# Moving the value products behind the side stages within each tick of a recurrent attention kernel

## The chip, the cores and the metric

The kernel runs on one core of a Trainium2 chip, as one program. The metric is the device time of one execution in microseconds. TensorE is called PE here, VectorE DVE, ScalarE ACT, GpSimd POOL and SyncE SP, as in the profile. PE's clock is granted at one of two levels, 1.2 or 2.4 GHz, which the profile shows as 0.5 or 1.0.

## The reference

The input is x, 16 sequences of 256 tokens with 128 features, all float32. Two layers each compute x = x + s * silu(g), where s is an attention and g a feed-forward stage of the normalized x.

```python
# layer 0
xn = layernorm(x)
s = attention0(xn)        # causal softmax attention, 16 heads of 64, then Wo and bo
g = silu(moe0(xn))        # one of 8 experts per token by a router, F = 352, plus a shared expert
x = x + s * g
# layer 1
xn = layernorm(x)
s = linear_attention(xn)  # 16 heads of 8, phi = elu + 1, cumulative sums of k*v over the tokens
g = silu(local_transformer(xn))
x = x + s * g
# local_transformer: 2 layers; token shift, qkv (8 heads of 64), l2norm of q and k, rotary with
# scale, softmax over a window of 64 and its predecessor, wo, residual; then
# token shift, layernorm, GLU with gelu (341), down projection, residual
```

## The kernel before

Tokens lie on the 128 partitions. Two sequences (512 tokens, four tiles of 128) make a block; there are 8 blocks. Both softmax attentions are cut into steps. A step is one pair of heads (`i`, 0 to 3), one sequence of the block (`s`, 0 or 1) and one part (half of the heads, or layer). Two steps with the same `i` make a pair. There are 256 steps in a plan of 361 ticks that is laid out when the kernel is built. Some ticks have no step, because the next layer's input isn't there yet.

A step passes through a pipeline of ticks. In tick T, PE makes the q of the pair that starts in T+2 and the k of the pair that starts in T+1 (`produce`, L488 or L498), the logits of step T (L508, L511), the transposes of the probabilities of step T-1 (L519) and the value products of step T-2 (`values`, L534, L537). If that was the second step of its pair, PE also transposes the expanded reciprocal sums, so that they lie as the output does (`merge`, L544). DVE masks and scales the logits and takes the maximum (L921), copies the transposed probabilities (L932), inverts the sums (L938) and multiplies the values by the reciprocals (`scaled`, L943), the last one tick later. ACT copies q and k (L758), takes the exponentials (L780, L781) and copies the spread of the reciprocals (`merge`, L758, tile rT). POOL expands the reciprocals (L1220).

All other work is in side stages, which the plan puts on ticks: `route` and the experts (`eT` L592, `eg` L603 and L608, `ed` L618), the value projection `v` (L479), the output projection `wo` (L562), the shared expert (`ffn`, `down0` L577, `comb`), and for layer 1 `xT`, `lin` (L630 on PE, L1070 and L1071 on DVE), `qkv` (three matmuls of 128x512 for one tile, L636; ACT squares and copies the first two banks, L836 and L837, DVE sums the squares, L1108, and applies the tables, L1113, POOL does L1302 and L1303, DVE `rot` L1118, then `rr`), `cum` (the cumulative sums: L645 and L647 on PE, L1086 and L1089 on DVE), `oT`, `s1`, `shift`, `ln2`, `yT`, `glu` (L682 and L684, ACT L858, DVE L1136), `down1` (L691, DVE L1142), `hT` and `fin` (L1148 to L1152). On every engine a tick is the attention's pipeline steps followed by the tick's side stages, with one exception that the change is about: where in this order `values` and `merge` stand.

The order of each engine's work is its program order, written out by the loops over the ticks. Engines wait for each other by semaphores. PSUM's eight banks are four rings of two: mm (q, k, the spread, and those side results that ACT reads), s (the logits, and side results that DVE reads), pt (transposed probabilities) and o (the value products). `count_units` walks the plan once and numbers the uses of each ring. A use waits until the use two before it in its ring was read. These numbers have to follow the order in which PE and the readers do the work, which is why `count_units` is changed with the loops.

Of the kernel before, what the change touches and what calls it, by code (L numbers as in the profile page):

```python
# [401 lines left out]
def count_units(c, plan):  # L402

    mm, s, pt, o = (Ring(f, d, 2) for f, d in ((c.mm_full, c.mm_done), (c.s_full, c.s_done),
                                                (c.pt_full, c.pt_done), (c.pv_done, c.o_done)))
    rings = {"mm": mm, "s": s, "pt": pt}
    for i in range(BLOCKS):
        mm.add(("rT", i))
    for t in range(TILES):
        mm.add(("v", 0, 0, t))  # L410
    mm.add(("q", 0))
    mm.add(("k", 0))
    o.add(("scores",))
    o.add(("cum",))
    plan.combs, combs = {}, 0
    for tick in range(plan.length):
        if plan.starts(tick + 2):
            mm.add(("q", plan.step(tick + 2).pair))
        if plan.starts(tick + 1) and tick:
            mm.add(("k", plan.step(tick + 1).pair))  # L420
        if st := plan.step(tick):
            for h in range(2):
                s.add(("s", st.n, h))
        if st := plan.step(tick - 1):
            for h in range(2):
                pt.add(("t", st.n, h))
        if st := plan.step(tick - 2):
            if st.s == 0:
                o.add(("o", st.pair))
            else:  # L430
                mm.add(("m", st.pair))
        for seg in plan.side.get(tick, ()):
            for ring, n in USES.get(seg[0], {}).items():
                for j in range(n):
                    rings[ring].add((*seg, j))
            plan.combs[seg] = combs
            combs += seg[0] == "comb"
    return mm, s, pt, o


# [12 lines left out]
def tensor(nc, pe, c, plan, mm, s, pt, o):  # L453
    MM, LAST = nc.tensor.matmul, PAIRS - 1

    def mm_bank(*name):
        if mm.free(*name):
            pe.wait_ge(c.mm_done, mm.free(*name))
        return c.mm_ps[mm.slot(*name)]
# [22 lines left out]
    def produce(which, st):  # L482
        bank = mm_bank("qk"[which], st.pair)
        if st.kind == 0:
            a = (st.part * PAIRS + st.i) * P
            if st.part == 0 and st.i == 0 and which == 0:
                pe.wait_ge(c.mm_done, mm.done("rT", st.b) if st.b < 2 else mm.done("xnT", st.b, 0))
            MM(bank[:, :], c.wqk[which][:, a:a + P], c.xnT[:, st.b % 2, :], start=True, stop=True).then_inc(c.mm_full, 1)  # L488
        else:
            if st.i == 0:  # L490
                g = LAYERS * st.b + st.part
                if which == 0:
                    pe.wait_ge(c.rot_ready, TILES * (g + 1))
                else:
                    pe.wait_ge(c.kn_ready, TILES * (g + 1))
            a = which * INNER1 + st.i * P
            for t in range(TILES):
                last = nc.tensor.transpose(bank[:, t * P:(t + 1) * P], c.qkr[:, t, a:a + P], c.ident[:, :])  # L498
            last.then_inc(c.mm_full, 1)

    def logits(st):
        if st.s == 0:
            pe.wait_ge(c.mm_done, mm.done("k", st.pair))
        banks = [s_bank("s", st.n, h) for h in range(2)]
        q, k = (c.qk[a][:, st.pair % 2, st.s * SEQ:(st.s + 1) * SEQ] for a in range(2))
        for h in range(2):
            f = HD * h
            MM(banks[h][:, 0:P], q[f:f + HD, 0:P], k[f:f + HD, 0:P], start=True, stop=True)  # L508
        for h in range(2):
            f = HD * h  # L510
            MM(banks[h][:, P:SB], q[f:f + HD, P:SEQ], k[f:f + HD, :], start=True, stop=True).then_inc(c.s_full, 1)  # L511

    def transposes(st):
        for h in range(2):
            u = 2 * st.n + h
            bank = pt_bank("t", st.n, h)
            pe.wait_ge(c.exp_done, u + 1)
            for j in range(3):
                last = nc.tensor.transpose(bank[:, j * P:(j + 1) * P], c.p[:, u % 4, j * P:(j + 1) * P], c.ident[:, :])  # L519
            last.then_inc(c.pt_full, 1)  # L520

    def values(st):
        bank = c.o_ps[o.slot("o", st.pair)]
        if st.s == 0:
            pe.wait_ge(c.o_done, o.free("o", st.pair))
            if st.i == 0:
                pe.wait_ge(c.mm_done, mm.done("qkv", st.b, st.part, LAST, 2) if st.kind else mm.done("v", st.b, st.part, LAST))
        v = (c.v0, c.v1)[st.kind][:, st.part, :, :]
        pe.wait_ge(c.pt_done, pt.done("t", st.n, 1))
        pts = [c.pt[:, (2 * st.n + h) % 4, :] for h in range(2)]  # L530
        q = st.s * SEQ
        for h in range(2):
            f, a = HD * h, st.i * P + HD * h
            MM(bank[f:f + HD, q:q + SEQ], v[:, 2 * st.s, a:a + HD], pts[h][:, 0:SEQ], start=True, stop=False)  # L534
        for h in range(2):
            f, a = HD * h, st.i * P + HD * h
            last = MM(bank[f:f + HD, q + P:q + SEQ], v[:, 2 * st.s + 1, a:a + HD], pts[h][:, SEQ:SB], start=False, stop=True)  # L537
        last.then_inc(c.pv_done, 1)

    def merge(pair):  # L540
        bank = mm_bank("m", pair)
        pe.wait_ge(c.rdx_ready, pair + 1)
        for t in range(TILES):
            last = nc.tensor.transpose(bank[:, t * P:(t + 1) * P], c.rdx[:, pair % 2, t * P:(t + 1) * P], c.ident[:, :])  # L544
        last.then_inc(c.mm_full, 1)
# [182 lines left out]
    for tick in range(plan.length):  # L728
        if plan.starts(tick + 2):
            produce(0, plan.step(tick + 2))  # L730
        if plan.starts(tick + 1) and tick:
            produce(1, plan.step(tick + 1))
        if plan.step(tick):
            logits(plan.step(tick))
        if plan.step(tick - 1):
            transposes(plan.step(tick - 1))
        if st := plan.step(tick - 2):
            values(st)
            if st.s == 1:
                merge(st.pair)  # L740
        if tick == 4:
            pe.wait_ge(c.wo_loaded, 16 * 2)
            pe.wait_ge(c.sh_loaded, 16 * 4)
            pe.wait_ge(c.p1_loaded, c.P1_LOADS)
        for seg in plan.side.get(tick, ()):
            if seg[0] in stage:
                stage[seg[0]](*seg[1:])


def scalar(nc, act, c, plan, mm, s, pt, o):  # L750
# [6 lines left out]
    def evacuate(dst, *name):  # L757
        A(dst, mm_bank(*name)[:, :], ACT.Copy).then_inc(c.mm_done, 1)  # L758
# [11 lines left out]
    def produce(which, st):  # L770
        evacuate(c.qk[which][:, st.pair % 2, :], "qk"[which], st.pair)

    def exps(st):
        if st.s == 0 and st.pair >= 2:
            act.wait_ge(c.rden_ready, st.pair - 1)
        for h in range(2):
            u = 2 * st.n + h
            act.wait_ge(c.s_done, s.done("s", st.n, h))
            den, p = c.den[:, st.pair % 2, 2 * st.s + h, :], c.p[:, u % 4, :]
            A(p[:, 0:P], p[:, 0:P], ACT.Exp, bias=c.nmax[:, u % 4, 0:1], scale=-1.0, accum_out=den[:, 0:1])  # L780
            A(p[:, P:SB], p[:, P:SB], ACT.Exp, bias=c.nmax[:, u % 4, 1:2], scale=-1.0, accum_out=den[:, 1:2])\  # L781
                .then_inc(c.exp_done, 1)

    def merge(pair):
        if pair >= 2:
            act.wait_ge(c.o_done, o.done("o", pair - 2))
        evacuate(c.rT[:, pair % 2, :], "m", pair)
# [89 lines left out]
    for tick in range(plan.length):  # L877
        if plan.starts(tick + 2):
            produce(0, plan.step(tick + 2))
        if plan.starts(tick + 1) and tick:  # L880
            produce(1, plan.step(tick + 1))
        if plan.step(tick):
            exps(plan.step(tick))
        if (st := plan.step(tick - 2)) and st.s == 1:
            merge(st.pair)
        if tick == 4:
            act.wait_ge(c.p1_loaded, c.P1_LOADS)
            act.wait_ge(c.hT_zero, 1)
        for seg in plan.side.get(tick, ()):
            if seg[0] in stage:  # L890
                stage[seg[0]](*seg[1:])


def vector(nc, dve, c, plan, mm, s, pt, o):
# [619 lines left out]
```

## Time and profile before

| | |
|---|---|
| median of 3 runs | 2476.11 us (2475.27 to 2476.41) |
| profiled execution | 2475.04 us |
| span in its profile | 2473.2 us |
| PE busy | 1920.5 us, 78% |
| DVE busy | 1487.3 us, 60% |
| ACT busy | 1093.3 us, 44% |
| POOL busy | 626.2 us, 25% |
| mean granted clock of PE | 0.888 |

The profile is one execution on the chip. Busy time is summed over an engine's instructions. A gap in front of an instruction is put down to the semaphore event that ended it, and the name behind `<-` is the instruction that raised it. In the timeline an engine's instructions of the same line are merged into one row; its first number is the start from the beginning of the span, its second the duration. The idle time in brackets is that ahead of the row's first instruction.

### The profile page before, as it was taken

What the parts mean: (1) busy time and instruction counts of PE and PEld (TensorE: products, weight loads), DVE (VectorE), ACT (ScalarE), POOL (GpSimd) and SP (SyncE); (2) the same over time, 40 slices, a digit from 0 to 9 for tenths busy, and PEclk for the clock granted to TensorE, in tenths of its full rate; (3) what the DMA queues carried; (4) which work ended last, traced back from release to release, by engine and by line L of the source; (5) the groups of instructions that cost most, each with busy time, mean ns of one, the idle gap of its engine ahead of it and who ended that gap; (6) DMA issues with size and microseconds to landing.
All of it is one profiled execution on the core that took longest, in us unless ns stands there. A gap on an engine that the chain in (4) does not pass through costs nothing.

```text
span 2473.2 us, 34580 instructions
## 1 busy us (share of the span) xinstructions
PE 1920.5 (78%) x11092; PEld 1219.0 (49%) x11092; DVE 1487.3 (60%) x4595; ACT 1093.3 (44%) x3143; POOL 626.2 (25%) x656
## 2 busy tenths in 40 slices
PE   5699977987689777887688676887699767866756
PEld 4377744554346445545355344544455435533524
DVE  4355557656665675646665656656666666566655
ACT  2355545454444454454344443454354444344334
POOL 2722223222411331131410323122321231034120
PEclk9799998998889898898889888998899788978878
DMA  7244300000000000000000000000000000000000
GB/s 215 79 153 159 116 8 1 1 5 1 1 9 1 5 1 1 9 1 5 0 10 1 5 1 1 9 1 1 1 10 1 1 1 5 1 5 0 5 1 5
DMA packets 46542, 51.69 MB, mean 21 GB/s; under 512 B 6290, under 2 KB 39068, under 8 KB 46364
## 3 DMA queue, kind: packets, MB, share of 16 engines
q0 software_dynamic: 7808, 27.79, 3.4%
q1 hardware_dynamic: 38556, 21.69, 3.1%
q8 instruction: 92, 1.51, 0.3%
q14 instruction: 86, 0.70, 0.1%
HBM read 40.03 MB, written 9.44 MB: 20 GB/s over the span
## 4 chain that ended last, share of the span: by engine, by line
PE 53%; DVE 19%; issue 12%; ACT 8%; POOL 7%; DMA 1%; DVEq 0%; SPq 0%; POOLq 0%; another core or an unknown queue 0%; ACTq 0%
PE ps L519 6%; PE ps L511 5%; PE ps L562 5%; PE ps L508 5%; PE ps L534 4%; PE ps L488 3%; PE ps L636 3%; DVE ss L1108 2%; PE ps L544 2%; PE ps L479 2%; PE ps L682 2%; POOL big L1206 2%; PE ps L691 2%; PE ps L645 2%; PE ps L684 2%
## 5 line engine op out<-in xcount | busy, mean ns | idle before, releaser
L780 ACT ACTIVATE p<-p,nmax 128x128 f32<-128x128 f32 x512 | 201.7, 394 | 531.6 <-DVE nmax L921 527.4
L1220 POOL COPY rdx<-rden 128x256 f32<-128x256 f32 x256 | 96.0, 404 | 1146.6 <-DVE rden L938 1117.8
L508 PE MATMUL ps<-k,q 64*128 64x128 f32 x1024 | 142.2, 355 | 227.7 <-DVE big L1086 102.1
L921 DVE CUSTOM_DVE_ANT_0 p<-ps,mask 128x128 f32<-128x128 f32 (+1 forms) x512 | 152.7, 354 | 217.1 <-PE ps L511 194.3
L921 DVE CUSTOM_DVE_ANT_0 p<-ps,mask,nrq 128x128 f32<-128x128 f32 (+1 forms) x512 | 183.2, 414 | 153.3 <-PE ps L511 153.1
L932 DVE COPY pt<-ps 128x384 f32<-128x384 f32 x512 | 260.8, 550 | 19.8 <-PE ps L519 19.7
L508 PEld LDWEIGHTS ps<-k,q 64*128 64x128 f32 x1024 | 91.8, 210 | 358.3 <-issue 182.5
L519 PE MATMUL ps<-ident,p 128*128 128x128 f32 x1536 | 260.4, 312 | 6.6 <-DVE ff L969 3.9
L781 ACT ACTIVATE p<-p,nmax 128x256 f32<-128x256 f32 x512 | 252.2, 493 | 0.0
L519 PEld LDWEIGHTS ps<-ident,p 128*128 128x128 f32 x1536 | 191.3, 157 | 111.7 <-issue 102.2
L636 PE MATMUL ps<-wqkv,hT 128*128 128x512 f32 x384 | 207.2, 645 | 49.5 <-ACT big L837 47.7
L498 PE MATMUL ps<-ident,big 128*128 128x128 f32 x512 | 94.9, 318 | 174.9 <-POOL big L1206 94.2
L1302 POOL TENSOR_TENSOR big<-big,rots 128x512 f32<-128x512 f32 x64 | 133.2, 2081 | 329.2 <-DVE ss L1108 329.2
L534 PE MATMUL ps<-pt,v 128*64 128x256 f32 x1024 | 187.2, 448 | 0.0
L511 PE MATMUL ps<-k,q 64*128 64x256 f32 x1024 | 182.7, 430 | 0.0
L498 PEld LDWEIGHTS ps<-ident,big 128*128 128x128 f32 x512 | 71.0, 165 | 207.7 <-issue 198.5
L758 ACT ACTIVATE q<-ps 128x512 f32<-128x512 f32 x128 | 76.0, 594 | 202.6 <-PE ps L498 114.5
L758 ACT ACTIVATE k<-ps 128x512 f32<-128x512 f32 x128 | 75.9, 593 | 181.5 <-PE ps L498 130.9
L1108 DVE TENSOR_REDUCE ss<-big 128x16 f32<-128x1024 f32 x64 | 77.9, 1217 | 105.7 <-ACT big L837 105.7
L562 PE MATMUL ps<-wo,attT 128*128 128x128 f32 x1024 | 133.8, 295 | 8.8 <-DVE attT L943 8.8
L636 PEld LDWEIGHTS ps<-wqkv,hT 128*128 128x128 f32 x384 | 62.7, 195 | 154.8 <-ACT big L837 102.6
L562 PEld LDWEIGHTS ps<-wo,attT 128*128 128x128 f32 x1024 | 132.3, 212 | 13.3 <-issue 12.4
(208 smaller groups left out, 3800.2 us busy)
## 6 DMA issues: line engine op xcount, KB each, us to landing
slots_in<-xn SPq DMA_DIRECT2D x1, 2560.0 KB, 14.0
v<-slots_in SPq DMA_DIRECT2D x20, 128.0 KB, 4.8
slots_out<-v SPq DMA_DIRECT2D x20, 128.0 KB
big<-in_x SPq DMA_DIRECT2D x4, 512.0 KB, 6.1
x<-in_x SPq DMA_DIRECT2D x8, 256.0 KB, 3.9
out_x<-x SPq DMA_DIRECT2D x8, 256.0 KB, 2.3
wqkv<-in_wqkv SPq DMA_DIRECT2D x2, 768.0 KB
g<-in_g SPq DMA_DIRECT2D x2, 341.0 KB
```

Of the source, the lines that this page charges most:

```text
L498: last = nc.tensor.transpose(bank[:, t * P:(t + 1) * P], c.qkr[:, t, a:a + P], c.ident[:, :])
L508: MM(banks[h][:, 0:P], q[f:f + HD, 0:P], k[f:f + HD, 0:P], start=True, stop=True)
L511: MM(banks[h][:, P:SB], q[f:f + HD, P:SEQ], k[f:f + HD, :], start=True, stop=True).then_inc(c.s_full, 1)
L519: last = nc.tensor.transpose(bank[:, j * P:(j + 1) * P], c.p[:, u % 4, j * P:(j + 1) * P], c.ident[:, :])
L534: MM(bank[f:f + HD, q:q + SEQ], v[:, 2 * st.s, a:a + HD], pts[h][:, 0:SEQ], start=True, stop=False)
L562: last = MM(bank[:, t * P:(t + 1) * P], c.attT[kind][:, i, t * P:(t + 1) * P], w, start=i == 0, stop=i == LAST)
L636: MM(bank[:, :], c.hT[:, t * P:(t + 1) * P], c.wqkv[:, l, i * INNER1:(i + 1) * INNER1], start=True, stop=True).then_inc(c.mm_full, 1)
L758: A(dst, mm_bank(*name)[:, :], ACT.Copy).then_inc(c.mm_done, 1)
L780: A(p[:, 0:P], p[:, 0:P], ACT.Exp, bias=c.nmax[:, u % 4, 0:1], scale=-1.0, accum_out=den[:, 0:1])
L781: A(p[:, P:SB], p[:, P:SB], ACT.Exp, bias=c.nmax[:, u % 4, 1:2], scale=-1.0, accum_out=den[:, 1:2])\
L921: last = V.tensor_tensor_reduce(out=c.p[:, u % 4, a:b], in0=bank[:, a:b], in1=c.mask[st.kind][:, P * (1 - i):SEQ], scale=scale, scalar=3e3 ...
L932: V.tensor_copy(c.pt[:, u % 4, :], bank[:, 0:SB]).then_inc(c.pt_done, 1)
```

## The change

On PE, `values` and `merge` are issued at the end of a tick, behind the side stages, and no longer ahead of them. On ACT, the copy of the spread moves behind the side stages too. In `count_units` the spread's number in the mm ring is given out behind those of the tick's side stages; the value products' ring (o) has the same order as before. DVE, POOL and SP are as they were: DVE's `scaled` still runs one tick after `values`, and POOL still expands the reciprocals at the start of its tick.

```diff
@@ count_units
-        if st := plan.step(tick - 2):
-            if st.s == 0:
-                o.add(("o", st.pair))
-            else:
-                mm.add(("m", st.pair))
+        if (st := plan.step(tick - 2)) and st.s == 0:
+            o.add(("o", st.pair))
         for seg in plan.side.get(tick, ()):
...
             combs += seg[0] == "comb"
+        if (st := plan.step(tick - 2)) and st.s:
+            mm.add(("m", st.pair))
@@ tensor
             transposes(plan.step(tick - 1))
-        if st := plan.step(tick - 2):
-            values(st)
-            if st.s == 1:
-                merge(st.pair)
         if tick == 4:
...
         for seg in plan.side.get(tick, ()):
             if seg[0] in stage:
                 stage[seg[0]](*seg[1:])
+        if st := plan.step(tick - 2):
+            values(st)
+            if st.s == 1:
+                merge(st.pair)
@@ scalar
             exps(plan.step(tick))
-        if (st := plan.step(tick - 2)) and st.s == 1:
-            merge(st.pair)
         if tick == 4:
...
                 stage[seg[0]](*seg[1:])
+        if (st := plan.step(tick - 2)) and st.s == 1:
+            merge(st.pair)
```

## Rows read from the trace of the kernel before

**Rows 1.** The page: PE's busy share, the chain by engine, PE's 40 slices.
```profile
PE 1920.5 (78%) x11092; PEld 1219.0 (49%) x11092; DVE 1487.3 (60%) x4595; ACT 1093.3 (44%) x3143; POOL 626.2 (25%) x656
...
PE   5699977987689777887688676887699767866756
...
PE 53%; DVE 19%; issue 12%; ACT 8%; POOL 7%; DMA 1%; DVEq 0%; SPq 0%; POOLq 0%; another core or an unknown queue 0%; ACTq 0%
```

**Rows 2.** Waits of the whole run: total us, times, longest us.
```profile
DVE ss L1108 <- ACT big L837: 105.7, 44, 4.3
...
PE ps L508 <- DVE big L1086: 102.1, 43, 7.0
...
PE ps L508 <- DVE v L1071: 68.5, 29, 3.8
...
PE ps L636 <- ACT big L837: 47.7, 54, 5.6
...
PE ps L508 <- DVE ff L1136: 5.6, 6, 0.9
...
PE ps L488 <- ACT xnT L758: 5.1, 6, 1.2
...
PE ps L508 <- DVE xb L1142: 2.2, 5, 0.4
```

**Rows 3.** Groups by line: busy us, mean ns, then idle us ahead.
```profile
L534 PE MATMUL ps<-pt,v 128*64 128x256 f32 x1024 | 187.2, 448 | 0.0
...
L544 PE MATMUL ps<-ident,rdx 128*128 128x128 f32 x512 | 89.6, 301 | 8.2 <-POOL rdx L1220 7.4 <-ACT hT L764 0.2
L943 DVE TENSOR_TENSOR attT<-ps,rT 128x512 f32<-128x512 f32 x128 | 82.9, 648 | 2.0 <-ACT rT L758 1.8
```

**Rows 4.** Timeline of ticks 115 and 116, first-layer qkv projection, block 2.
```profile
889.66 0.87 PE L519 MATMUL ps<-ident,p 128*128 128x128 f32 x6
...
890.47 0.65 PE L534 MATMUL ps<-pt,v 128*64 128x256 f32 x4
...
891.76 3.38 PE L636 MATMUL ps<-wqkv,hT 128*128 128x512 f32 x6
...
892.30 0.57 ACT L758 ACTIVATE rT<-ps 128x512 f32<-128x512 f32 x1
892.88 0.60 ACT L836 ACTIVATE big<-ps 128x512 f32<-128x512 f32 x1
...
895.21 1.22 DVE L1108 TENSOR_REDUCE ss<-big 128x16 f32<-128x1024 f32 x1 [3.10 <-ACT big L837]
...
899.64 0.80 PE L508 MATMUL ps<-k,q 64*128 64x128 f32 x4 [3.85 <-DVE v L1071]
...
901.22 1.54 PE L519 MATMUL ps<-ident,p 128*128 128x128 f32 x6
...
904.74 0.60 ACT L836 ACTIVATE big<-ps 128x512 f32<-128x512 f32 x1 [0.73 <-PE ps L636]
...
906.84 1.22 DVE L1108 TENSOR_REDUCE ss<-big 128x16 f32<-128x1024 f32 x1 [1.19 <-ACT big L837]
```

**Rows 5.** Timeline of ticks 138 and 139: value products, GLU, the next logits.
```profile
1058.67 0.65 PE L534 MATMUL ps<-pt,v 128*64 128x256 f32 x4
...
1059.47 1.11 PE L682 MATMUL ps<-xT,g 128*114 128x512 f32 x2
...
1065.81 0.49 PE L508 MATMUL ps<-k,q 64*128 64x128 f32 x4 [0.93 <-DVE ff L1136]
```

**Rows 6.** Timeline rows of ticks 8, 129 and 149.
```profile
118.44 0.66 PE L592 MATMUL ps<-ident,v 128*128 128x128 f32 x2 [12.74 <-DMA v<-slots_in]
...
996.13 0.80 PE L508 MATMUL ps<-k,q 64*128 64x128 f32 x4 [6.21 <-DVE big L1086]
...
1155.32 0.69 DVE L974 TENSOR_TENSOR ff<-ps,xn 128x512 f32<-128x512 f32 x1 [1.99 <-PE ps L577]
```

**Rows 7.** Windows view, PE alone: us, busy us (instructions), granted clock, DMA share, GB/s.
```profile
899.40:902.80 3.40, 3.16 (x16) 0.50 0.00 0
```

## The prediction

> **What bounds the kernel now.** I read the views in this order: the page's busy shares and chain, the totals of who waited for whom, the groups by line, and then single ticks in the timeline. TensorE (PE) is busy 78% of the span and holds 53% of the chain that ended last; in the third to fifth slice of the page it is at 9 tenths [rows 1]. That is the expert stage (ticks 9 to 29): PE has no idle time there, so an order that does the same work cannot gain in it. Elsewhere PE idles some 550 us in all (2473.2 less 1920.5). The reader is to see in the totals where it idles: at the logits of the next tick, L508, for a scores bank that VectorE (DVE) has not yet emptied of a side stage's result, 102.1 us behind the cumulative sums (L1086) and 68.5 us behind the linear attention's projection (L1071); and inside the qkv projection (L636), 47.7 us for ScalarE's (ACT) copies. DVE in turn waits 105.7 us for ACT's copies of that projection before L1108 [rows 2]. So PE, DVE and ACT hand one side stage to each other, and the tick ends when that relay ends. Against this stand the value products and their spread: L534 has 0.0 us of waits ahead of it over 1024 instructions, L544 has 8.2 us over 512, and DVE's consumer L943 waits 2.0 us over 128 [rows 3]. They are ready early and wanted late: filler that now stands ahead of the relay.
>
> **What moves.** In every tick PE's value products (0.80 us from L534's start to the next stage's, 1058.67 to 1059.47) [rows 5], and in every second one also the four transposes of the spread (1.29 us together, 890.47 to 891.76) [rows 4], go behind the side stages; ACT's copy of the spread, 0.57 us [rows 4], goes behind ACT's side stages; and the ring of matmul banks is numbered anew. No instruction is added or removed, no DMA is issued in the moved code, DVE's, POOL's and SP's orders stay. PE's work between two logits is the same, so a tick can only gain where PE, DVE or ACT waited for the side stage, and can only lose where the side stage, now earlier by 0.80 or 1.29 us, meets something that isn't ready and the filler no longer covers it.
>
> **First-layer qkv projection (4 ticks in each of 8 blocks).** Rows 4 show two of them. In the first, transposes end at 890.53. ACT's exponentials end at 892.30, then comes the spread's copy, and the projection's first copy L836 starts at 892.88. After the change the first bank is full by about 891.6 (one of the three in 3.38 us), so L836 can start at 892.30: 0.58 us earlier, and DVE's L1108, which waited 3.10 us, with it, and so the logits at 899.64, which waited 3.85 us for the last DVE step of the tick. PE itself ends later: its third bank needs the first one's copies, then filler follows, by my count at 5.9 us behind the transposes where it is 5.3 now; the 3.85 us hide that. In the second tick L836 waits 0.73 us for PE and L1108 1.19 us for ACT: 0.73 us gained [rows 4]. The third repeats the first, the fourth is bound by DVE and POOL: nothing. Per block 0.58 + 0.73 + 0.58 = 1.9 us, times 8 = 15 us (between 1.2 and 3 us per block, since the same ticks at half clock have more room: 10 to 24).
>
> **Second-layer projection (7 blocks with steps around it).** DVE waits on average 105.7 / 44 = 2.4 us in front of L1108 [rows 2], in the first of those ticks with the value products ahead; everything behind runs DVE, POOL, DVE. One 0.80 us each: 5.6 us (0 to 9).
>
> **Smaller relays.** The GLU tick ends in a wait of 0.93 us of the logits, with value products of 0.80 us ahead of the GLU [rows 5]; such waits sum to 5.6 us, those behind the down projection to 2.2 us, those of the next q for xnT's copy to 5.1 us, of which about 3.6 us have filler to cover them [rows 2]. Together 11.4 us. Behind the cumulative sums 43 waits make 102.1 us, but some 15 of them are of the kind of 996.13: 6.21 us, because DVE has 6 us of other work (the block's output) queued ahead of L1086, which the change doesn't touch [rows 2, 6]; 102.1 - 15 x 6.21 leaves 9 us, of which I take half, 4.5 us. Behind L1071, 15 of 29 are those of 3.85 us already counted [rows 2, 4]; of the remaining 11 us I take 2.5. Where the attention output and the shared down projection share a tick (the tick of 1155.32) DVE waits 1.99 us at L974, and then has three long steps before the next scores [rows 6]; 1.3 us in each of five such ticks: 6.5 us. Sum of gains: 15 + 5.6 + 11.4 + 4.5 + 2.5 + 6.5 = 45.5 us.
>
> **Losses.** (1) In the ten value-projection ticks outside the expert stage (L479, the shape of L636), PE fills two banks in 2.0 us behind the transposes, but ACT's exponentials end 1.77 us behind them and its first copy 0.6 us later [rows 4]: 0.4 to 0.5 us of wait that the filler covered, 5 us in all (0 to 13: with all 1.29 us lost). (2) The first expert transposes wait 12.74 us for a DMA, with value products ahead [rows 6]. They will run behind it, at half clock: 1.2 us (0.8 to 1.6). (3) A cumulative sum's bank is freed by DVE's first scores, some 0.1 us later than PE will come in about 20 ticks: 3 us (0 to 5). (4) Where yT is transposed, the next q or k waits for yT's copy instead of the spread's, 0.2 us x 7 = 1.4 us. Together 10.6 us. The delayed copy of the spread itself costs nothing: its reader L943 runs behind the next tick's scores and copies; if that cover were gone, it would be the side stage's length on DVE.
>
> **The sum.** 45.5 - 10.6 = 35 us. The profiled execution took 2475.04 us (span 2473.2), 1.1 us under the median of 2476.11; the difference carries over: 2476.1 - 35 = 2441 us.
>
> **Rivals.**
> (a) *The clock adds to it.* The stretch behind the 3.85 us wait is granted 0.50, the 1.2 GHz level [rows 7], and the six transposes there take 1.54 us where they took 0.87 a tick earlier [rows 4]. Filler in those waits makes them shorter by 1.3 us. If the clock then stays at 2.4 GHz, each such stretch gives back half of its 3.16 us of work, 1.6 us; two per block: 16 x 1.6 = 25 us more, 2416 us. The Trainium skill (TensorE: Matmul & The Clock Gate, "HAM oscillation") says that idle gaps between bursts throttle the array, and counts the penalty as half the throttled time; by that rule the trace agrees in the stretch shown, and the time would be this rival's. Against it: the waits that remain are still 2.5 to 6 us. Chance 0.15.
> (b) *Swallowed.* The gains meet DVE's or POOL's long steps later in the block (as at 996.13) and only a third arrives: 15 - 10.6 = 5 us, 2471 us. For it: DVE is busy 60% of the span and is what L508 waits for. Chance 0.15.
> (c) *Slower: the projection ticks become PE's.* In some 44 qkv ticks PE now stalls ahead of the third bank, because ACT is still in the exponentials, and does its filler afterwards, 0.65 us later per tick (5.9 against 5.3 above): 28 us, plus 10.6 us of losses, less the 25 us of gains outside the projections = +14 us, 2490 us. It decides if the wait that follows such a tick is under 0.65 us; for the ticks in rows 4 it is 3.85 us, which speaks against it. Chance 0.10.
> (d) *Nothing.* PE's idle time only moves within the tick, because DVE is the bound wherever PE waits: 2476 us. DVE's waits in rows 2 and 4 speak against it. Chance 0.05.
>
> **Numbers.** Forecast 0.55, and (a) to (d) as given. The range from 2408 to 2471 us takes in the forecast with the bounds of its terms (gains of 25 to 65 us, losses of 2 to 21), (a), and (b) to its edge; out are (c), (d) and the tails. A measurement of this kernel can tell about 0.2%, 5 us, from no change. Faster by more: 0.55 + 0.15 + 0.11 of (b) = 0.81. Same: 0.04 of (b) and (d) = 0.09. Slower: 0.10.
>
> **What would show it.** Right: L508's waits behind L1071 fall from 68.5 us by some 15, DVE's ahead of L1108 from 105.7 by 20; L534 and L544 follow the side stage and fill the start of the waits; L508's waits of 0.93 behind L1136 are gone; the L508 wait of 6.21 stays. PE's busy time falls only if (a) holds. Wrong: L636's waits for ACT (47.7 us) grow by more than 30 us while the waits behind those ticks vanish, which is (c); or the waits of L498 for DVE and POOL grow by what L508's fall, which is (b).

## The result and the profile after

The changed kernel takes 2445.18 us, the median of 4 runs (2444.57 to 2447.01), against 2475.87 us for the kernel before on the same chip (4 runs, 2475.27 to 2476.41): a ratio of 0.9881, 95% interval 0.9868 to 0.9893. It is 30.7 us faster; the forecast was 35 us faster, 2441 us. The profiled execution has a span of 2443.5 us. One run of the kernel before, with a mean granted clock of 0.71, took 2725.22 us and is left out of every comparison. The line numbers of the kernel after are one lower than those of before from `count_units` on: logits L507 and L510, transposes L518, value products L533 and L536, the spread L543, the qkv projection L635. In the kernels of the experiments the same lines have other numbers still; the operation and the tiles tell which they are.

The page: PE's busy time and its share, its 40 slices, and the chain by engine, as in [rows 1].

```profile
PE 1924.6 (79%) x11092; PEld 1212.7 (50%) x11092; DVE 1484.4 (61%) x4595; ACT 1092.7 (45%) x3143; POOL 624.8 (26%) x656
...
PE   5699987986689787888679777987698767866857
...
PE 53%; DVE 18%; issue 12%; ACT 10%; POOL 6%; DMA 1%; DVEq 0%; SPq 0%; POOLq 0%; ACTq 0%
```

PE has no less to do than before (1924.6 against 1920.5 us busy): the 30 us came out of its idle time. The third to fifth slice, the expert stage, are at 9 as they were.

Waits of the whole run (total us, times, longest us), to be read against [rows 2]:

```profile
DVE ss L1107 <- ACT big L836: 77.8, 45, 3.0
...
PE ps L497 <- POOL big L1205: 93.9, 16, 7.7
PE ps L507 <- DVE big L1085: 90.1, 20, 6.8
...
PE ps L497 <- DVE big L1117: 73.5, 16, 9.7
...
PE ps L635 <- ACT big L836: 56.7, 63, 5.5
...
PE ps L507 <- DVE v L1070: 45.9, 23, 2.8
...
PE ps L681 <- ACT ff L857: 4.6, 7, 0.7
```

The logits' waits behind the linear attention (L1070) fell from 68.5 to 45.9 us, DVE's ahead of the squares (L1107) from 105.7 to 77.8, the logits' behind the cumulative sums (L1085) from 102.1 to 90.1. The last row, PE's third GLU matmul behind ACT's gelu, is new. The moved instructions by line (busy us, mean ns, idle ahead), against [rows 3]:

```profile
L533 PE MATMUL ps<-pt,v 128*64 128x256 f32 x1024 | 179.7, 432 | 0.0
...
L543 PE MATMUL ps<-ident,rdx 128*128 128x128 f32 x512 | 86.8, 294 | 8.7 <-POOL rdx L1219 8.5
L942 DVE TENSOR_TENSOR attT<-ps,rT 128x512 f32<-128x512 f32 x128 | 82.7, 646 | 6.9 <-ACT rT L757 6.8
```

The value products still wait for nothing. The late copy of the spread costs its reader 6.9 us where it was 2.0. Ticks 115 and 116 in the timeline, against [rows 4]:

```profile
884.66 1.88 PE L635 MATMUL ps<-wqkv,hT 128*128 128x512 f32 x4
...
886.59 0.58 ACT L835 ACTIVATE big<-ps 128x512 f32<-128x512 f32 x1
...
887.70 1.12 PE L635 MATMUL ps<-wqkv,hT 128*128 128x512 f32 x2 [1.16 <-ACT big L836]
...
888.64 1.22 DVE L1107 TENSOR_REDUCE ss<-big 128x16 f32<-128x1024 f32 x1 [2.25 <-ACT big L836]
...
889.40 0.65 PE L533 MATMUL ps<-pt,v 128*64 128x256 f32 x4
...
890.96 0.60 ACT L757 ACTIVATE rT<-ps 128x512 f32<-128x512 f32 x1 [1.19 <-PE ps L543]
...
893.07 0.49 PE L507 MATMUL ps<-k,q 64*128 64x128 f32 x4 [2.21 <-DVE v L1070]
...
897.39 0.60 ACT L835 ACTIVATE big<-ps 128x512 f32<-128x512 f32 x1 [0.49 <-PE ps L635]
...
899.49 1.22 DVE L1107 TENSOR_REDUCE ss<-big 128x16 f32<-128x1024 f32 x1 [0.95 <-ACT big L836]
```

Here the step is seen whole. ACT goes from its exponentials straight to the projection; PE waits 1.16 us ahead of the third bank, the products and the spread come behind, and the logits of tick 116 still wait, 2.21 us instead of 3.85. Tick 115 lasts from its first logits (883.10) to those of tick 116 (893.07), 9.97 us; before it was 10.84 (888.80 to 899.64). It is 0.87 us shorter.

I did this for all ticks: the start of a tick's first logits in the trace of before, less that in the other trace, is the lead, and what the lead gains from one tick to the next belongs to the tick between. It compares one profiled execution of each kernel. In the kernel after the lead ends at 29.9 us, made up (rounded) of the following; where two numbers stand, the second is of the stretches that run from such a tick over the ticks without a step behind it (there logits don't mark the ticks):

| ticks | lead gained, us | term of the forecast |
|---|---|---|
| first-layer qkv projection, with the gaps behind it | 19.1 - 1.2 | +15 |
| second-layer projection, fourth tick (6) | 5.6 | +5.6 |
| GLU with cumulative sums (7) | -3.2 | GLU +5.6 in all |
| GLU without sums (6, +2.9 of it) and other stretches without steps, the first three ticks of the second-layer projection among them (6 blocks, -2.1 of it) | +6.2 | |
| down projection (13) | -3.4 | +2.2 |
| other ticks with cumulative sums (73) | -5.0 | +4.5 - 3.0 |
| value projection without sums: ticks 14, 21, 91, 212 | +1.2 | -5 (for the ten outside the expert stage) |
| shared expert (8) | +1.8 | +6.5 |
| ticks 0 to 9, first expert transposes among them | -0.8 | -1.2 |
| linear attention alone (15) | +1.2 | +2.5 |
| the 79 others (46 of them without side stages on PE and ACT, +6.3 of it) | +8.5 | xnT and yT, +3.6 - 1.4 |

### The profile page after: what moved, and what is told of

It is laid out like the page before. It is cut to its first block, busy times and chain, and to the rows that moved or that the text cites. A ratio compares the mean times of both kernels' runs of the same rounds, so it can differ in the third digit from the quotient of the medians.

```text
span 2443.5 us, 34579 instructions
## 1 busy us (share of the span) xinstructions
PE 1924.6 (79%) x11092; PEld 1212.7 (50%) x11092; DVE 1484.4 (61%) x4595; ACT 1092.7 (45%) x3143; POOL 624.8 (26%) x656
## 4 chain that ended last, share of the span: by engine, by line
PE 53%; DVE 18%; issue 12%; ACT 10%; POOL 6%; DMA 1%; DVEq 0%; SPq 0%; POOLq 0%; ACTq 0%
PE ps L561 5%; PE ps L518 5%; PE ps L510 5%; PE ps L507 4%; PE ps L533 4%; PE ps L487 4%; ACT p L780 2%; DVE ss L1107 2%; PE ps L644 2%; ACT p L779 2%; PE ps L497 2%; PE ps L478 2%; PE ps L543 2%; PE ps L635 2%; PE ps L690 2%
## 5 line engine op out<-in xcount | busy, mean ns | idle before, releaser
L507 PE MATMUL ps<-k,q 64*128 64x128 f32 x1024 | 140.9, 353 | 178.9 <-DVE big L1085 90.1
L931 DVE COPY pt<-ps 128x384 f32<-128x384 f32 x512 | 260.6, 550 | 23.2 <-PE ps L518 23.1
L518 PE MATMUL ps<-ident,p 128*128 128x128 f32 x1536 | 259.6, 311 | 5.6 <-ACT p L780 3.8
L635 PE MATMUL ps<-wqkv,hT 128*128 128x512 f32 x384 | 204.8, 645 | 59.5 <-ACT big L836 56.7
L518 PEld LDWEIGHTS ps<-ident,p 128*128 128x128 f32 x1536 | 190.9, 157 | 105.7 <-issue 98.3
L507 PEld LDWEIGHTS ps<-k,q 64*128 64x128 f32 x1024 | 89.1, 207 | 294.6 <-issue 155.0
L497 PE MATMUL ps<-ident,big 128*128 128x128 f32 x512 | 96.4, 321 | 169.3 <-POOL big L1205 93.9
L510 PE MATMUL ps<-k,q 64*128 64x256 f32 x1024 | 180.9, 430 | 0.0
L533 PE MATMUL ps<-pt,v 128*64 128x256 f32 x1024 | 179.7, 432 | 0.0
L497 PEld LDWEIGHTS ps<-ident,big 128*128 128x128 f32 x512 | 67.5, 163 | 193.2 <-issue 188.1
L757 ACT ACTIVATE rT<-ps 128x512 f32<-128x512 f32 x128 | 76.0, 593 | 172.9 <-PE ps L543 172.4
L635 PEld LDWEIGHTS ps<-wqkv,hT 128*128 128x128 f32 x384 | 67.6, 203 | 162.6 <-ACT big L836 112.3
L561 PE MATMUL ps<-wo,attT 128*128 128x128 f32 x1024 | 139.5, 302 | 7.0 <-DVE attT L942 7.0
L561 PEld LDWEIGHTS ps<-wo,attT 128*128 128x128 f32 x1024 | 136.9, 218 | 13.1 <-issue 10.3
```

The lines of the kernel that those rows point to most:

```text
L561: last = MM(bank[:, t * P:(t + 1) * P], c.attT[kind][:, i, t * P:(t + 1) * P], w, start=i == 0, stop=i == LAST)
L635: MM(bank[:, :], c.hT[:, t * P:(t + 1) * P], c.wqkv[:, l, i * INNER1:(i + 1) * INNER1], start=True, stop=True).then_inc(c.mm_full, 1)
L931: V.tensor_copy(c.pt[:, u % 4, :], bank[:, 0:SB]).then_inc(c.pt_done, 1)
```

## The experiments

In each experiment a function of the tick's side stages says whether `values` and `merge` (on PE and ACT, and in `count_units`) stand early, as before, or late, as after. The rest is as in the kernel after.

**The projection ticks alone, and all the others alone.**

```diff
+    kinds = {seg[0] for seg in plan.side.get(tick, ())}
+    late = bool(kinds & {"qkv", "lin"})          # e1; e2: not kinds & {"qkv", "lin"}
```

> Value products and spread stand behind the side stages only in ticks whose side stages hold a qkv or lin projection (both layers); in all other ticks they stand ahead, as before. Theory (the relay: the gain comes from ACT and DVE getting the projection earlier): the lead of the changed kernel grows by 17.6 us in the ticks with lin and qkv and some 5 us in those with qkv alone, so 2476 - 24 = 2452 us, and since the small losses of other ticks are gone perhaps 2447. Rival (the clock: the gain comes from filler breaking up idle time anywhere): about half of the gain, 2460 us. Rival (swallowed elsewhere): 2470 us or more.

> The complement: value products and spread stand behind the side stages in every tick except those with a qkv or lin projection. Theory (relay): what is left are gains of some 12 us (GLU ticks without a step, xT, value projection at the start, the ticks around block 0) and losses of some 12 us (cumulative sums with GLU or down projection, the first expert transposes), so 2474 us, within 0.3% of the kernel before. Rival (clock): 2460 us. If the forecast's own small terms (11.4 + 4.5 + 6.5 - 10.6 us) were right: 2464 us.

Measured: e1 2445.88 us (ratio 0.9884, 0.9867 to 0.99), e2 2475.26 us (1.0, 0.9991 to 1.001). All of the gain is in the ticks with a projection or the linear attention. In the others, gains and losses cancel: in the trace of e2 the GLU with sums loses 3.3 us and the down projection 3.4, as in the kernel after. The forecast's smaller terms, taken together, are not there.

**Which of the two moved parts does it.** e4 moves the value products alone (spread and its copy early), e5 the spread and its copy alone.

```diff
+    return 1, 0          # values late, spread early: e4; e5: return 0, 1
```

> In every tick the value products stand behind the side stages, but the spread's transposes stay ahead of them on PE and its copy stays ahead of them on ACT. Theory (relay): in the odd projection ticks ACT's copy of 0.57 us stays in front of the projection's copies, which is what bounded them there, so about 0.6 us x 16 to 20 odd ticks with a projection of the gain is lost; even ticks keep theirs: 2445 + 11 = 2456 us. Rival (PE's order alone makes the gain; ACT's copy is covered): 2447 us.

> The value products stay ahead of the side stages in every tick; only the spread's transposes on PE and its copy on ACT go behind them. Relay theory: what is gained in a projection tick is ACT's 0.57 us (and PE's 0.6 us) ahead of the first projection copy, so the ticks with the spread (the one of rows 4 at 884 to 891 us) gain 0.6 to 0.9 us as in the full change, and the tick without it (0.73 us in rows 4, where only the value products stand ahead) gains nothing: 8 ticks x 0.9 x 1 to 2 = 7 to 14 us, and the losses of the moved products are gone. With the value products alone moved giving 20 us (2455.6) and both giving 30 us, the two parts should be roughly additive: 2475.6 - 10 to 16 = 2460 to 2466. Rival, the parts are not additive because one delay in the tick hides the other: 2471 to 2475.

Measured: e4 2455.57 us (0.9923, 0.9906 to 0.994), e5 2472.75 us (0.9989, 0.9979 to 0.9999). The products alone give 20 us, the spread alone 3, both together 30.7: they are not additive. e5 missed its expectation and fell into the rival's range. With the products still ahead, the spread gains 3.8 us in the first-layer projection ticks, and the stretches without steps behind them lose 10.2 us. In the one behind tick 117 (ticks 117 to 121) PE is busy 22.8 us where it was 19.4 us before, at a granted clock of 0.73 where it was 0.79. So much of that loss is the clock's; whether the order made the clock fall is not shown.

**The first-layer projection alone.**

```diff
+    late = any(seg[0] == "qkv" and seg[2] == 0 for seg in plan.side.get(tick, ()))
```

> Values and spread late only in the 32 ticks that carry the first-layer qkv projection. Sized in the forecast at 15 us, against 5.6 for the second layer; the late order in all projection and linear-attention ticks gave 29.7 us. Theory from the lead of tick against tick: 10.2 + 7.3 us from the two ticks per block that also hold the linear attention, about 4 + 2 from the others of the same projection: 2475.6 - 22 = 2453 (2450 to 2457). Rival, the forecast's own split (second layer and linear attention carry the rest, 14 us): 2460.

Measured: 2463.72 us (0.9954, 0.9936 to 0.9972), 12 us faster, not 22, and below the forecast's 15. In its trace the late ticks gain 17.2 us, less 1.5 in the gaps behind them, as they should; the rest is lost again in ticks whose order is that of before. The mean granted clock of its four runs is 0.883 to 0.885, against 0.886 to 0.889 in the kernel before.

**The losing ticks early, and they alone late.** e3 keeps the early order where there are cumulative sums, a down projection, a value projection, yT or the first expert transposes; e8 has the late order only there.

```diff
+    if kinds & {"qkv", "lin", "xnT"}:
+        late = True
+    elif kinds & {"glu", "down1", "cum", "v", "yT"} or kinds == {"eT", "wg", "xs"}:
+        late = bool(kinds & {"glu"}) and not kinds & {"cum"}
+    else:
+        late = True
```

> Behind the side stages in ticks with qkv, lin or xnT, in GLU ticks without cumulative sums and in ticks with none of the following; ahead of them in ticks with cumulative sums, down1, v, yT (none of them beside qkv or lin), and in the first expert tick. Theory (each tick's lead in the comparison of the two traces belongs to that tick's own order): the losses of 3.2 (GLU with sums), 2.3 + 1.7 (down1), 1.1 + 0.9 + 1.0 + 0.5 (sums, with wo, yT, v) and 1.0 us (first expert tick) go, so 2445 - 10 = 2435 us. Rival (the losses are only shifted starts that later waits give back): 2445 us.

> Values and spread late only in the ticks with cumulative sums, down projection of the second layer, value projection, yT or the first expert transposes, and early everywhere else. The kernel with the late order in all ticks but these took 2438.8, the one with it in all ticks 2445.2: if the ticks are independent this kernel takes 2475.6 + 6.4 = 2482 (2480 to 2485), and is the first one slower than before. Rival (the losses arise only because the gains elsewhere shift the phase of DVE and ACT against PE): 2474 to 2477.

Measured: e3 2438.78 us (0.9857, 0.9841 to 0.9874), e8 2491.53 us (1.0067, 1.0049 to 1.0085). The selection is worth another 6 us over the kernel after. e8 is slower by 15.8 us where 6.4 were expected: it is the right sign, and more than twice the size. Of the 15.7 us of lead that it loses, the first-layer projection ticks and the gaps behind them hold 15.1 (6.9 and 8.2), and in these the order is the one of before. What they differ in is seen in the windows view, PE alone (us, busy us, granted clock, DMA share, GB/s). Tick 78, tick 154, tick 191, the start of tick 117 and tick 243 of the kernel before:

```profile
626.50:638.20 11.70, 7.71 (x32) 0.86 0.01 2
1181.20:1193.00 11.80, 7.81 (x30) 0.85 0.00 0
1451.60:1463.80 12.20, 8.32 (x36) 0.81 0.00 0
...
911.30:918.00 6.70, 6.56 (x38) 1.00 0.00 0
...
1821.80:1827.70 5.90, 4.63 (x34) 1.00 0.15 44
```

Tick 78 of e8, with the same order of work:

```profile
629.20:642.30 13.10, 9.15 (x30) 0.76 0.01 2
```

It lasts 13.1 instead of 11.7 us: less of it is granted the 2.4 GHz level (0.76 against 0.86), and PE is busy 9.15 instead of 7.71 us with the same work. Ticks 116 and 230 do the same in e8, and the stretch of ticks 79 to 83 is 1.5 us longer at 0.75 against 0.79.

**Is it the clock's phase?** e12 takes the kernel before with its order untouched, and adds eight transposes in tick 17, in the expert stage, which makes that tick 0.87 us longer (9.02 for 8.15).

```diff
+        twice[0] = 2 * TILES * (tick in (17, 18))    # only tick 17 has a spread
...
-        for t in range(TILES):
+        for t in (*(t % TILES for t in range(twice[0])), *range(TILES)):
             last = nc.tensor.transpose(bank[:, t * P:(t + 1) * P], c.rdx[:, pair % 2, t * P:(t + 1) * P], c.ident[:, :])
```

> The kernel before with its order untouched; the spread of one pair in the expert stage (tick 17 or 18, where PE has no idle time) is transposed two times more, 8 transposes of 0.17 to 0.33 us, so everything behind starts 1.3 to 2.6 us later. It tests what was seen in the kernel with the late order in the rest only: ticks whose order is as before took up to 1.5 us more each because the clock rose later in them. Theory (where the clock falls and rises depends on where the ticks lie, and a shift alone moves single unchanged ticks by about 1.5 us): single ticks change by 1 us or more, both ways, and the total is off the plain 1.3 to 2.6 us by several us, anywhere from 2470 to 2490. Rival (each tick's time follows from its own order): all ticks behind keep their length to 0.1 us, and the total is 2477 to 2478.

Measured: 2474.67 us (0.9996, 0.9987 to 1.0005). The total did not move beyond its interval, but single ticks moved both ways, some by more than 1 us: the stretch of ticks 31 to 37 is 2.4 us shorter, tick 71 1.5 us shorter, tick 78 1.4 us longer. Most ticks behind tick 9 keep their length to 0.1 us. The test is not as clean as it was meant: ticks 2 to 9, where PE waits for POOL and for DMAs, already differ by up to 1.3 us each with the same order, so that tick 18 starts 1.46 us late and not 0.87. Behind the shorter stretch of ticks 31 to 37 everything starts early, tick 71 by 1.0 and tick 78 by 3.9 us. The windows of ticks 71 and 78 in e12:

```profile
582.30:586.80 4.50, 4.50 (x33) 0.76 0.00 0
...
622.60:635.70 13.10, 9.12 (x30) 0.76 0.01 2
```

Tick 71 took 6.00 us in the kernel before, with PE busy all of it at a clock of 0.54 (the row below, from its windows view). Tick 78 is e8's again, in a kernel whose order is that of before. So with shifts of one to four microseconds other work meets PE at 1.2 GHz, by 1.4 to 1.5 us in such a tick. There is one trace of each kernel, so that the runs don't tell whether the eight transposes made the shifts or an execution's own start did; that the order of these ticks did not is shown.

```profile
583.30:589.30 6.00, 6.00 (x32) 0.54 0.01 3
```

Here the changes nearly cancelled; in e8 they did not. The total's half of the expectation (several us off) did not come true.

**Filler in PE's stall.** In the kernel after, PE waits 56.7 us ahead of the third projection bank and fills in afterwards. e6 puts the value products between the second and the third matmul.

```diff
         for i in range(3):
+            if i == 2 and inside:
+                values(inside.pop())
             bank = mm_bank("qkv", b, l, t, i)
```

> As the kernel after, but in ticks with a qkv projection the value products stand between its second and third matmul, where PE waits for ACT to free the bank. It tests the forecast's slower rival (PE's stall ahead of the third bank, 0.65 us in some 44 ticks). Relay theory: PE's end of the tick is hidden behind DVE and POOL, and the third bank is not on that chain, so no change: 2445, +-2 us. Rival (PE's stall counts, swallowed in part by the gains): faster, by up to 44 x 0.65 = 28 us, and at least 5 us: under 2440.

Measured: 2451.93 us (0.9902, 0.9885 to 0.992). The groups view of e6 (busy us, mean ns, idle ahead) shows that the stall was filled, 37.2 us for 56.7:

```profile
L647 PE MATMUL ps<-wqkv,hT 128*128 128x512 f32 x384 | 209.1, 656 | 39.9 <-ACT big L855 37.2 <-ACT hT L782 2.7
```

It bought nothing, and the kernel is 6.7 us slower than the kernel after, outside either theory's range. The rival that PE's stall decides is out. In the first-layer ticks and the gaps behind them e6 leads by 16.7 - 3.1 us, against 19.1 - 1.2. That difference is one of the clock's size (tick 154 gained 1.8 us in the kernel after, and lost 0.3 in e6), but I did not separate it from what the order itself does.

**More filler in the wait.** e9 does the spread's transposes twice in the 15 ticks that have both a spread and a first-layer projection.

```diff
+        twice[0] = TILES * any(seg[0] == "qkv" and seg[2] == 0 for seg in plan.side.get(tick, ()))
...
-        for t in range(TILES):
+        for t in (*range(twice[0]), *range(TILES)):
```

> As the kernel after, but the four transposes of the spread are done twice (same operands, same bank, the second writes over the first) in the 15 ticks that carry both a spread and a first-layer qkv projection: 60 more transposes, 1.29 us at a time, 19 us of PE's work, put into the wait that stands ahead of the next logits (2.21 us in tick 115 of the kernel after). Relay theory: PE is not on the path behind the side stage, so nothing is lost: 2445, within 2 us. Clock rival: the shorter idle gap keeps the clock at its upper level in the next tick, which gives back up to 1.6 us a time: 2445 - 10 to 24, under 2436. Third case, the spread is on the path once it is late (its copy's reader, or the bank that the next q needs): 2445 + 10 to 19.

Measured: 2445.06 us (0.9878, 0.9861 to 0.9894), the time of the kernel after. Tick 115 in e9:

```profile
889.11 1.09 PE L553 MATMUL ps<-ident,rdx 128*128 128x128 f32 x8
...
891.98 0.49 PE L517 MATMUL ps<-k,q 64*128 64x128 f32 x4 [1.78 <-DVE v L1094]
```

Sixty more transposes cost nothing: PE isn't on the path there. They were less of a load than expected: the eight take 1.09 us where four took 0.66, so it is some 6 us in all (an estimate) and not 19. They also bought nothing in sum. The idle gap got a little shorter (here 1.78 us for 2.21), and tick 116 another 0.8 us, but not its like in the other blocks, and e10 below, without the added transposes, has the same short tick 116 (10.03 us in both, 10.84 in the kernel after). The first-layer ticks together lead by 19.8 us where it was 19.1.

**The loss in the GLU.** e10 puts the value products ahead of the third pair of GLU matmuls, which in tick 126 of the kernel after waits for ACT.

```diff
         for i, (f0, rows) in enumerate(GCHUNKS):
+            if i == 2 and inside:
+                values(inside.pop())
             bank = mm_bank("glu", b, l, i)
```

> As the kernel after, but in the 16 ticks with the GLU the value products stand ahead of its third pair of matmuls, which in the kernel after waits 0.66 us for ACT's gelu of the first bank (tick 126). Theory: in the 7 ticks that also carry cumulative sums this stall is what made them 0.46 us longer than before, so filler in it takes the loss back: those ticks end 0.4 us earlier each, 2445 - 3 = 2442. Rival (the loss has another cause, the sum's bank or DVE): those ticks keep their -0.46 us and the time stays at 2445; or, if the products there delay the third bank's own readers, 2446 to 2450.

The wait in the kernel after (timeline: tick 126; below it, for the section on the prediction, the logits of ticks 129 and 139, the down projection of tick 139, and tick 149):

```profile
966.66 1.11 PE L681 MATMUL ps<-xT,g 128*113 128x512 f32 x2 [0.66 <-ACT ff L857]
...
990.62 0.80 PE L507 MATMUL ps<-k,q 64*128 64x128 f32 x4 [5.80 <-DVE big L1085]
...
1059.39 0.49 PE L507 MATMUL ps<-k,q 64*128 64x128 f32 x4
...
1061.02 2.94 PE L690 MATMUL ps<-g,ff 114*128 114x128 f32 x24 [0.70 <-DVE nmax L920]
...
1148.40 0.69 DVE L973 TENSOR_TENSOR ff<-ps,xn 128x512 f32<-128x512 f32 x1 [1.99 <-PE ps L576]
```

The same tick in e10:

```profile
968.00 0.65 PE L543 MATMUL ps<-pt,v 128*64 128x256 f32 x4
...
968.80 1.11 PE L695 MATMUL ps<-xT,g 128*113 128x512 f32 x2
...
973.02 0.49 PE L517 MATMUL ps<-k,q 64*128 64x128 f32 x4 [0.35 <-DVE big L1110]
```

The mechanism is confirmed: the wait of 0.66 us is gone, and the seven ticks lose 0.0 us in place of 3.2. The kernel nevertheless takes 2450.52 us (0.99, 0.9884 to 0.9917), 5 us more than the kernel after. In the GLU ticks without sums the logits wait for the GLU's last bank; there the products inside stand ahead of it again, and each is 1.0 us longer than in the kernel after (one 2.0 us), which takes back what the late order had won.

**A better selection.** e11 changes e3 in five ticks: late in ticks 14, 21, 91 and 212 with value projections, early in tick 243.

```diff
+    if kinds & {"cum", "down1", "yT"} or kinds == {"eT", "wg", "xs"} or (kinds & {"xnT"} and kinds & {"kv"}):
+        late = bool(kinds & {"qkv", "lin"}) or {"xnT", "down1"} <= kinds
+    else:
+        late = tick != 5
```

> A second selection of the ticks with the late order: as in the selected kernel (2438.8 us), but late also with the value projections outside cumulative sums (ticks 14, 21, 91, 212; the trace of the kernel after shows no loss there, +0.9 us behind tick 212), and early in tick 243, which ended 1.5 us later there. Forecast from the trace: 2438.8 - 1.5 - 0.5 = 2437 (2435 to 2440), the best of the study. Rival, the single ticks are not independent and the last microseconds are chance of the clock's phase: 2439 to 2446.

Measured: 2438.82 us (0.9853, 0.9838 to 0.9868), no better than e3. The reason to change tick 243 was wrong. With the early order it is slower still, 8.4 us against 5.9 before:

```profile
1786.60:1795.00 8.40, 7.58 (x34) 0.62 0.10 31
```

PE does the same 34 instructions in 7.58 us at a clock of 0.62, where before it was 4.63 us at 1.00. I had read a change of the clock as a loss of the order.

## Why the prediction was right, and where it was not

**The time.** 2445.2 us lies inside the range, 4 us above the forecast, and the likeliest case is the one that came. PE's value products and spread were filler ahead of a relay of PE, ACT and DVE, and behind it they lie in a wait. e9 shows the last point at its strongest, e1 shows the place. That the sum came so near is in part luck, since the split was wrong. By the forecast the ticks with a projection or the linear attention were worth 23.1 us (15 + 5.6 + 2.5) and the others 11.8; e1 measured 29.7 us for the first, and e2 0.3 us, which is nothing, for the others.

**First-layer projection, forecast 15 us, measured 17.9.** The step for the first tick said 0.58 us from ACT's copy; it gained 0.87 (0.85 in six of the seven blocks behind the first). ACT starts its first projection copy 3.49 us behind the logits instead of 4.08, which is the 0.58, and the copies of the first two banks end another 0.28 us sooner. That I had missed; the spread held one of the two mm banks in the order before, so that the projection's second bank could be filled only behind the spread's copy. The trace of before shows that wait, in tick 115, ahead of PE's weight load for the second bank:

```profile
892.93 0.30 PEld L636 LDWEIGHTS ps<-wqkv,hT 128*128 128x128 f32 x2 [0.97 <-ACT rT L758]
```

The second tick: 0.73 forecast, 0.80 measured in the blocks without a change of clock. The third tick: 0.58 forecast, 0.0 measured. DVE's squares start 6.38 us behind the logits as they did before (6.40), since PE starts the tick at half clock now (the window below, against 1.00 in the row 911.30 of before). What made up for it is again the clock: ticks 154 and 191 were shorter by 1.8 and 2.1 us, and not by 0.8. Without a change of clock a block gives 0.85 + 0.80 us, some 13 us in eight blocks (an estimate); the other 5 of the 17.9 us came with a higher clock in ticks 154, 191, 192, 268 and 306 (0.77 to 0.84 in tick 192, for example), less what the stretches behind lost.

The windows of the kernel after, tick 116, tick 154, tick 191 and the start of tick 117:

```profile
893.10:903.90 10.80, 7.62 (x30) 0.84 0.01 2
1174.10:1184.10 10.00, 6.00 (x30) 0.98 0.00 0
1439.10:1449.10 10.00, 6.63 (x36) 1.00 0.00 0
...
903.90:910.60 6.70, 6.31 (x22) 0.75 0.00 0
```

So rival (a) came in single ticks (0.85 to 0.98, 0.81 to 1.00) and was taken back in others (1.00 to 0.75), and PE's busy time as a whole did not fall. The mechanism that I gave for it, that shorter gaps hold the clock, did not hold in e9. The Trainium skill (TensorE: Matmul & The Clock Gate, "Part 1: The HAM clock gate") says that how much of the work runs cold depends on where it lands against a monitor that runs on its own, that it varies from run to run, and that the cost of warming up is below 1% of a typical kernel. The size here is of that order: e8's 15 us are 0.6%. That it varies from run to run agrees too: the ten runs of e5 took 2469.3 to 2475.2 us, the four shortest at a mean granted clock of 0.891, the four longest at 0.886 to 0.887. But it is not all chance of a run: the four runs of e8 lie within 5 us of each other, and 11 us or more above the twelve runs of before that they are compared with.

**Second-layer projection, 5.6 forecast, 5.6 measured.** The agreement is luck. The forecast took 0.8 us in the first of these ticks, in seven blocks. Six blocks have steps around them, and the stretches without steps that hold the first three of the ticks are not shorter in sum but 2.1 us longer, three of them by 0.7 to 0.8 us. The 5.6 us are of the fourth tick, where three blocks gain 1 to 3 us; the largest, tick 220, took 10.28 us at a granted clock of 0.77 and takes 7.14 us at 1.00. e1 and e7 differ by 17.8 us in time, and the term is 5.6 of it.

**GLU and down projection, forecast +7.8, measured -3.7.** This is the step that failed in sign. The GLU ticks without sums did as said: the wait of 0.93 us is gone, the logits at 1059.39 wait for nothing, and the tick is 0.99 us shorter (2.9 us in all; five of the six gain, the last loses 0.9 at a granted clock of 0.89 instead of 1.00). But seven of the GLU ticks also carry cumulative sums, and there PE's own work ends the tick. Without filler ahead of it, PE reaches the third bank 0.66 us before ACT has freed it; ACT comes from the exponentials and loads a table ahead of the gelu, as its row in tick 126 of the kernel after shows. So the tick is 0.46 us longer, and e10 shows the cause.

```profile
964.62 1.28 ACT L857 ACT_TABLE_LOAD   x1
```

The down projection's bank is of the s ring; it is freed by DVE's scores, and PE now waits 0.70 us for them. I had listed this mechanism as loss (3), for the sums alone.

**Sums, forecast +4.5 and -3, measured -5.0.** The loss was about right, the gain isn't there. The wait of 6.21 us is 5.80 now: DVE's other work ahead of it sets it, as said, and I had no row for the half of the rest that I took.

**Shared expert, forecast 6.5, measured 1.8.** DVE's wait at L973 is 1.99 us in tick 149, as it was [rows 6], and tick 149 is only 0.54 us shorter. The step took the products for work ahead of L577 on a path that bounds DVE, but they are 0.65 us of PE's, and I took twice that and in five ticks. Of the 1.8 us, 1.7 are of tick 187, where PE is busy 6.83 instead of 8.24 us at a granted clock of 0.75 instead of 0.62.

**Value projection, forecast -5, measured +1.2.** The four ticks of the row are not the ten of the forecast, and tick 212 alone has 0.9 us of their gain. Tick 5 gains 5.5 us by the late order, because its value projection no longer stands behind a spread that waits 3.19 us for POOL, and all of it is given back by the logits of tick 8: in tick 7 the late spread waits 4.36 us for POOL (L543), which is issuing the DMAs of the scatter. In the ticks that also have cumulative sums the loss is 0.3 us at most, where I had counted 0.4 to 0.5.

**First expert transposes**, forecast -1.2: tick 8 is 1.0 us longer in the kernel after (18.60 for 17.56). That the order did it is not shown: e1, e7 and e12, which keep the early order there, took 18.4 to 18.5 us.

**The others**, forecast +2.2 for xnT and yT, measured +8.5, are no single term. 6.3 us of it are in the 46 ticks in which neither PE nor ACT has a side stage, so that the order of work is that of before. Part of it is the clock. Tick 205, which has no side stage on PE, took 5.4 us and takes 3.9 us now; its windows before and after:

```profile
1564.20:1569.60 5.40, 5.40 (x28) 0.68 0.34 100
```

```profile
1547.30:1551.20 3.90, 3.90 (x30) 1.00 0.45 134
```

That changes of this kind also come in ticks that no edit touches is what e12 shows; how much of the 8.5 us belongs to the order stays open.

**Signs named ahead.** L508's waits behind L1071 were to fall by 15 and fell by 22.6 us; L1108's by 20, and fell by 27.9. L636's waits grew by 9 us, under the 30 of rival (c), and e6 shows that they don't matter. Rival (b) is out: the waits of L498 for POOL and DVE were 94.2 and 80.2 us, those of L497 are 93.9 and 73.5. The late copy of the spread did not cost nothing: 4.9 us of waits of L942, though none of the path that I could find.

## What to carry to other kernels

Work that is ready early and wanted late belongs behind the stage whose result other engines hand on, but tick by tick: it pays where the tick ends in a wait for that relay, and costs where PE's own work ends the tick and the filler covered the time until a bank comes free. Moving it only where the trace shows the first kind gave 2438.8 us here, against 2445.2 for moving it everywhere. A gain of under 1% should be read tick by tick against the granted clock before it is put down to the order: a tick that changes by more than a microsecond at another clock tells nothing of the edit.

## What the runs showed of the hardware

In e12 single ticks that no edit touches, and that start about one to four microseconds off their place in the kernel before, changed by 1.1 to 1.6 us, in those looked at through the granted clock (tick 71 from 0.54 to 0.76, tick 78 from 0.86 to 0.76), and one tick of e11 by 2.5 us (1.00 to 0.62). In e8 such changes in the first-layer projection ticks and the gaps behind them added up to 15 us of 2476, and a median over more runs does not remove that: all four runs of e8 took 2489.8 us or more. Between the runs of one kernel the clock moves as well, by less: e5 took 2469.3 to 2475.2 us in ten runs, with mean granted clocks of 0.891 to 0.886.
